# Token gathers of a language-model kernel: three rounds ahead in place of two, and each of eight behind an event of its own

## The reference

```
h = take(tok_weight, x)                        # embedding rows of 128 floats, by token id
h = h + attn(layernorm(h))                     # linear attention, 8 heads of 16, per sequence of 256
...                                            # then: layernorm, softmax over 32 router columns,
...                                            # an expert layer, causal attention, a second expert layer
def attn(x):
    q, k, v = relu(x Wq), relu(x Wk), x Wv
    denom = clip(q . sum_n(k), 100)
    return ((q (k^T v * temperature)) / denom) Wproj + bproj
```

## Time and profile before

| | us |
|---|---|
| median of 3 runs | 2489.4 |
| lowest, highest run | 2485.23, 2490.82 |
| the profiled execution, first to last instruction | 2699.1 |
| its first stage, from the start to the end of the last round | some 407 |
| TensorE busy in it | 2356.4 |
| GpSimd busy in it | 1417.6 |

### The profile page before, as it was taken

The page is one execution under the profiler, slowest core; times in us unless marked ns, Lnnn a source line. Parts: engine busy times, 40 slices in busy tenths (PEclk is TensorE's granted clock), DMA queues, the critical chain, the costliest instruction groups (busy, mean ns, idle before and its releaser), DMA issues.

```text
span 2699.1 us, 59231 instructions
## 1 busy us (share of the span) xinstructions
PE 2356.4 (87%) x16796; PEld 2038.8 (76%) x16796; DVE 1876.1 (70%) x8463; ACT 1698.0 (63%) x5249; POOL 1417.6 (53%) x1724
## 2 busy tenths in 40 slices
PE   4888878676866669999999999999999999999976
PEld 3777765443434439999999998999989899999965
DVE  4666656654544437888888888777778898888733
ACT  3665654321211128787777777878778788888844
POOL 6333310055555536788778776444444476547443
PEclk9888889889988889999999999999999999999988
DMA  2554559233333343111111114655555688658577
GB/s 70 181 171 165 174 195 211 44 100 114 112 98 110 114 126 97 42 45 47 49 45 47 50 44 117 171 155 160 156 156 148 179 240 237 185 164 236 165 226 218
DMA packets 357907, 361.96 MB, mean 134 GB/s; under 512 B 35603, under 2 KB 301692, under 8 KB 357584
## 3 DMA queue, kind: packets, MB, share of 16 engines
q1 hardware_dynamic: 321376, 272.95, 36.7%
q0 software_dynamic: 33472, 78.98, 8.9%
q10 hardware_dynamic: 2736, 6.25, 0.7%
HBM read 208.38 MB, written 144.00 MB: 131 GB/s over the span
## 4 chain that ended last, share of the span: by engine, by line
PE 69%; DVE 11%; issue 8%; another core or an unknown queue 4%; ACT 3%; POOL 2%; DMA 1%; SPq 1%; ACTq 0%; DVEq 0%; POOLq 0%
PE bank L2190 7%; PE bank L2283 6%; PE bank L2269 6%; PE bank L2201 5%; PE bank L2189 4%; PE bank L2236 4%; PE bank L2244 4%; PE bank L2216 4%; PE bank L2218 4%; PE bank L2217 4%; PE bank L2159 3%; PE bank L2146 3%; PE bank L2127 2%; PE bank L1989 2%
## 5 line engine op out<-in xcount | busy, mean ns | idle before, releaser
L930 POOL DMA_INDIRECT zbuf<-pc,kb x248 | 252.2, 1017 | 232.5 <-DVE pc L1846 174.2
L924 POOL DMA_INDIRECT spread_rows<-kb,pos x248 | 252.9, 1020 | 196.8 <-DVE pc L1846 105.8
L2190 PE MATMUL bank<-xT,gT 128*128 128x256 f32 x1024 | 306.3, 381 | 0.0
L1649 DVE COPY pr_place<-bank 128x384 f32<-128x384 f32 x512 | 281.5, 550 | 16.6 <-PE bank L2201 13.9
L1628 DVE TENSOR_REDUCE nmax<-bank 128x1 f32<-128x128 f32 x512 | 144.3, 282 | 190.2 <-PE bank L2190 101.4
L1135 ACT ACTIVATE pr_place<-bank,nmax 128x128 f32<-128x128 f32 x512 | 188.9, 369 | 132.5 <-DVE nmax L1629 121.0
L2283 PE MATMUL bank<-wvo_part,x_part 128*128 128x512 f32 x768 | 268.2, 457 | 0.8 <-ACT vo_place L1223 0.8
L1145 ACT ACTIVATE bank<-causal 128x384 f32<-128x384 f32 x512 | 253.5, 495 | 19.4 <-PE bank L2374 3.3
L2201 PE MATMUL bank<-ident,pr_place 128*128 128x128 f32 x1536 | 252.2, 273 | 8.1 <-DVE pr_place L1649 7.9
L2201 PEld LDWEIGHTS bank<-ident,pr_place 128*128 128x128 f32 x1536 | 197.5, 141 | 74.4 <-issue 8.9
L2269 PE MATMUL bank<-x_part,wqk_part 128*128 128x256 f32 x1536 | 246.2, 296 | 1.2 <-DVE x_part L1789 1.2
(11 more groups left out here) (366 smaller groups left out, 6819.7 us busy)
## 6 DMA issues: line engine op xcount, KB each, us to landing
pa<-bundle SPq DMA_DIRECT2D x196, 321.0 KB
table<-rows SPq DMA_DIRECT2D x96, 576.0 KB
rows<-table SPq DMA_DIRECT2D x192, 128.0 KB
wu_more<-bundle SPq DMA_DIRECT2D x65, 321.0 KB
kb<-spread_rows SPq DMA_DIRECT2D x248, 65.0 KB
junk<-zbuf SPq DMA_DIRECT2D x31, 512.0 KB
h3buf<-h SPq DMA_DIRECT2D x64, 128.0 KB
kb<-kb SPq DMA_DIRECT2D x31, 256.0 KB
```

What stands on the lines that cost most here:

```text
L924: pool.indirect_dma_start(out=spread_rows, out_offset=bass.IndirectOffsetOnAxis(ap=pos[:, k, j:j + 1], axis=0), in_=xr4s[g % 2][:, k, j], ...
L930: pool.indirect_dma_start(out=zbuf, out_offset=bass.IndirectOffsetOnAxis(ap=xu_at(t)[:, C + 1:XW].bitcast(U32), axis=0), in_=yu[:, t % YR] ...
L1649: dve.tensor_copy(prT[:, h % 2], t_bank(u)[:, 0:3 * P]).then_inc(prT_ready, 1)
L2190: pe.matmul(s2[:, P:3 * P], g[:, P:2 * P], xT3[:, p], start=False, stop=True, skip_group_check=True)\
```

## The change

GpSimd's gathers of the first stage run three rounds ahead (round i+3 in round i) and no longer two; one more round's gathers stand ahead of the rounds. Inside the rounds, each of the eight indirect DMAs has a wait of its own and a `nop` ahead of it, for the event that `point(i, k)` gives: k from 0 to 3 for the first group, 4 to 7 for the second.

```diff
+            def point(i, k):
+
+                return ((xT_ready, 2 * i + 1), (kv_ready, 8 * i + 4), (q_ready, 2 * i + 1), (md_ready, 2 * i + 1),
+                        (md_ready, 2 * i + 2), (xn_ready, 2 * i + 3), (o_ready, 2 * i + 1), (oT_ready, 2 * i + 2))[k]
+
-            def gather(g, w, p):
+            def gather(g, w, p, i=None):
...
                 for j in range(TG):
+                    if i is not None:
+                        pool.wait_ge(*point(i, TG * p + j))
+                        pool.nop(nofuse=True)
                     pool.indirect_dma_start(out=xg_at(g)[:, j], out_offset=None, in_=L0_tok_weight,
...
-            for p in range(2):
-                gather(2 + p, 1, p)
+            for i in (1, 2):
+                for p in range(2):
+                    gather(2 * i + p, i % 2, p)
 
             def one(v, w):
                 i = 2 * v + w
-                if within(i + 2):
+                if within(i + 3):
                     for p in range(2):
-                        gather(2 * (i + 2) + p, w, p)
+                        gather(2 * (i + 3) + p, 1 - w, p, i)
```

## The result

| | median us | lowest, highest | ratio to before, 95% interval |
|---|---|---|---|
| before | 2489.35 | 2485.23, 2490.82 | |
| after | 2474.67 | 2473.87, 2478.95 | 0.9945 (0.9932 to 0.9957) |

The change makes the kernel 14.7 us faster, 0.55%. The direction was forecast and the time lies in the range, but the gain is 14.7 us where 32 were forecast.

The account below looks back on a forecast made before the run. The first stage was taken as bound by hand-overs between TensorE, VectorE and ScalarE, slowed by late signals during gathers. Terms 35.8 + 6.1 - 2.5 = 39 us, discounted to 32, gave 2489.4 - 32 = 2457 us; range 2434 to 2491.

Parts of the forecast that it names:

- the sum: Whole kernel: 35.8 + 6.1 - 2.5 = 39 us less than the profiled 2699.1; 32 taken off the median 2489.4.
- the case without late signals: Rival, chance 0.17: late signals mostly the profiler's; first-stage rounds already some 18.4 us, 11 gained at best, nearer 3: 2486.
- the term of 35.8 us: Rounds 2 to 12: spaced gathers let TensorE's late signals pass, 23.34 to 20.09 us a round; bounds 0 to 68.
- the other use of being ahead: First stage: VectorE's statistics no longer wait for same-round gathers; GpSimd's loop would keep rounds near 18.4 us; counted for nothing.
- round 12: Trace of before: GpSimd paused 2.04 us ahead of its second gather, called an accident; 20.09 us, used to price spacing.
- The statistics of gathered rows: Round 14 lacks them; round 13, which keeps those of round 15's rows, was put at 18.4 us, between 17.15 and 20.09.
- the feedback: Rounds with gathers: late signals hold the next gathers back, the backlog drains and signals pass; the burst lacks this.
- One sign of the mechanism: Round 9's end: the next clip starts 1.43 us later, at 254.99, read as a wait for a finished matmul.
- Round 13 and round 1: First stage: round 13, without gathers, 6.1 us less; round 1, with eight for round 4, 2.5 us more (0 to 6).
- The waits cost nothing: GpSimd: six more waits with `nop`, 2.8 us a round, fit in 2.9 us of room ahead of the copy of probabilities.
- The rival of disturbance over the whole round: Chance 0.13: each spaced gather still holds a signal by 1.43 us; rounds 24.8, 28.5 at worst; 13 us slower, 2502.
- The rival by the Trainium skill: First stage: by the skill's rule no gather makes TensorE's products late; spreading brings nothing, time stays at the median.

Follow-up runs that it names:

- e5: Kernel before, unedited, profiled on chip 6, where TensorE's signals aren't late: 2486.1 us with the profile, 2487.6 in the median of seven.
- e0: Kernel before, unedited, profiled again on chip 5, where TensorE's signals are late: 2714.0 us; 17 runs there have a median of 2702.8.
- e6: Against the kernel before, on chip 6: gathers three rounds ahead, eight in a row without waits of their own: 2472.6 us, ratio 0.9945.
- e2: Against the kernel before, on chip 5: still two rounds ahead, each gather behind its event: 2665.9 us, ratio 0.9851.
- e3: The changed kernel, unedited, against the kernel before on chip 5: 2637.5 us, ratio 0.9759.

## Why the prediction was right or wrong

**The step that failed is the sum, in its transfer to the median.** It set 39 us against 2699.1 and carried 32 of them to 2489.4, "since the waits are real for the engines". They are real, but in executions such as those of chip 5, and the timed runs weren't of that kind. The difference of 209.7 us, noted and laid to an unknown place or the profiler, goes with the chip: the same kernel was timed at 2702.8 on chip 5 and at 2485 to 2488 on 6 and 15. Its size was a warning to give the case without late signals far more than 0.17. On the quiet chip the late signals, the term of 35.8 us, are worth nothing (e5's masks and clips wait at most 0.5 us). What was gained there is the wait for gathered rows, a term for which the prediction counted nothing. Rounds 2 to 13 are shorter by 12 x (18.40 - 17.18) = 14.6 us; with the first copy 1.35 us later, the stage ends 13.3 us earlier (its last copies start at 341.72 in e5 and 328.46 in the changed kernel). That is nearly all of the measured 14.7; the other 1.4 us are not placed.

**The mechanism of the quiet chip was in the prediction,** under "the other use of being ahead": a line from GpSimd's copy through gathers, landing, statistics and residual, 18.4 us. e5's rounds are 18.40, but the agreement is luck. The prediction's line goes through all eight gathers, as round 12 of its trace does, where the eighth starts at 325.28 and the statistics 3.47 us later. e5's goes through the first four, whose rows take some 6.7 us. The loop was counted for nothing, because on the trace at hand the late signals came first; and in the rival that used it, the floor without it was put at 17.5 and the gain at 11 us at best, nearer 3. The floor is 17.18. The statistics of gathered rows, for which I added up to 1.25 us, hide in VectorE's waits for TensorE: the changed kernel's rounds with them are as long as the earlier trace rows's round 14 without them.

**On the late-signal chip the mechanism was right and its price too small.** The term of 11 x (23.34 - 20.09) = 35.8 used round 12, whose pause was no accident: e0 and e5 have the same 2.04 us ahead of the same gather, and e0's round 12 takes 20.46 us beside its mean of 23.64, a second sign that a gap in the line helps. The changed kernel's rounds 2 to 13 there take 215.51 / 12 = 17.96 us, from 23.64: 68 us in the stage, 65 in the medians, where the sum was 39. The eight waits do more than that one gap; that it is by the feedback (a late mask holds the next gather) is argued, as no run took the feedback from the spacing. The clock went from 0.87 to 1.00 with it.

One sign of the mechanism was misread: the 1.43 us from the clip at 253.56 to the next at 254.99 is VectorE's own work between them. In the trace of before, round 9 and round 14:

```profile
252.12 0.17 DVE L1363 TENSOR_SCALAR den<-bank 128x16 f32<-128x16 f32 x1 [0.94 <-PE bank L2011]
...
253.77 0.35 DVE L1367 RECIPROCAL den<-den 128x32 f32<-128x32 f32 x1
254.16 0.89 DVE L1372 TENSOR_TENSOR pr_place<-bank,den 128x128 f32<-128x128 f32 x4
...
364.61 0.17 DVE L1363 TENSOR_SCALAR den<-bank 128x16 f32<-128x16 f32 x1 [0.29 <-PE bank L2011]
```

Without any gather the same step takes 366.01 - 364.61 = 1.40 us. But the masks and clips at 249.19, 250.68, 252.12 and 253.56, each behind a wait, are 1.44 to 1.49 us apart, so the spacing of the signals stands by these.

**Round 13 and round 1.** Forecast 6.1 less and 2.5 more. On the late-signal chip round 13 went from 360.96 - 337.28 = 23.7 to 17.2 us, 6.5 less. On the quiet chip the first copy moved from 71.45 to 72.80, 1.35 us later.

**The waits cost nothing:** right on the quiet chip. e6 without them and the changed kernel with them have one ratio, 0.9945, and 2.42 us are left ahead of the copy where 2.9 were forecast.

**The rival of disturbance over the whole round** is refuted on both kinds of chip: no version with spaced gathers three rounds ahead has rounds over 17.96 us. **The rival by the Trainium skill** (SBUF — State Buffer, "Who interferes with whom") took the page's rule that DMA never contends with a compute engine, and that PE and ACT never wait on anyone, to mean that spreading would bring nothing. On the quiet chip that is what e6 shows, spacing adds nothing; on the late-signal chip e2 shows 37 us for spacing alone, against that reading. The page speaks of ports, and no run shows whether the late signals have to do with any. In neither did its time, the median of before, come out, since the gain on the quiet chip is no contention but a wait for data.

**Shown and argued.** Shown: which part brings what on the quiet chip, that being ahead alone brings nothing that can be told on the other, and that late signals go with unspaced gathers there. Only argued: that a signal waits for a gather of a backlog to land, and that the rows of the first group wait for the stores. What differs between the chips, or between the occasions, and whether lines of two or four suffice on the late-signal one, is open; no version that was run beats the changed kernel on either.

## What to carry to other kernels

When a profiled execution is 8% longer than the timed runs, don't scale: first get a second profile, or make the gap a case with a large chance and a sum of its own. A prefetch issued in the round that consumes it closes a loop through the issuing engine's other work; add up that loop (copy, issues, landing, consumer) even where something else seems to come first. Spacing indirect DMAs behind events of the chain costs nothing on a quiet chip once they are a round further ahead, costs 1% there if they are not, and on the chip with late signals it took off 1.5% by itself and 2.4% together with the distance.

## What the runs showed of the hardware

The runs on chips 5 and 6 have one program 8.7% apart (2702.8 and 2486.4 us). In the changed kernel the spans are 2629.7 us (e3, chip 5) and 2477.2 (the profile of the result). Of the difference of 152.5 us the first stage has 14 (its last copies start at 342.54 and 328.46). The expert stage, in which GpSimd issues its gathers in lines of four, has 105 from the first gather of rows to the second attention's first softmax: 941.3 - 467.3 = 474.0 us on the one,

```profile
L903 POOL DMA_INDIRECT rows<-table,idx x128: 950/968/1323, 467.3 to 901.0; - x128
...
L1144 ACT ACTIVATE pr_place<-bank,nmax x512: 358/367/408, 941.3 to 2495.3; 128x128 f32<-128x128 f32 x171
...
467.30:941.30 474.00, 326.23 (x1565) 199.26 (x1565) 217.50 (x878) 94.01 (x156) 253.16 (x256) 0.85 0.36 111
```

and 822.3 - 453.6 = 368.7 us on the other:

```profile
L903 POOL DMA_INDIRECT rows<-table,idx x128: 952/971/1309, 453.6 to 787.2; - x128
...
L1144 ACT ACTIVATE pr_place<-bank,nmax x512: 357/367/407, 822.3 to 2354.9; 128x128 f32<-128x128 f32 x171
...
453.60:822.30 368.70, 292.52 (x1565) 181.37 (x1565) 216.05 (x878) 94.01 (x155) 254.40 (x256) 0.95 0.46 143
```

The first two lines of each give the shortest, median and longest duration in ns, and the first and last start in us; the third is the stretch by engine, as in the earlier trace rows. The instructions of VectorE, ScalarE and GpSimd take the same time on both chips (busy 217.50 and 216.05, 94.01 and 94.01, 253.16 and 254.40 us). TensorE's same 1565 matmuls are busy 34 us longer on chip 5, at a granted clock of 0.85 and not 0.95. The other 71 us are idle time of TensorE (474.00 - 326.23 beside 368.70 - 292.52). Whether the lower clock comes from the waits or is a cause of its own is open. The stretch of the second attention's softmaxes is 21 us longer on chip 5 (1554.0 and 1532.6), and what follows it 12.
